# Graph attention with residual and layer norm on one core: node features cut on chip by ScalarE, and fewer, longer transfers for codes and run ends

## The chip, the cores and the metric

The kernel runs on one core of one Trainium2 chip. The metric is the device time of one execution in microseconds. Three runs of the kernel before took 2470.12 to 2475.89 us, the median is 2471.67 us.

## The reference

A graph of N = 6250 nodes with 128 features each and E = 200,000 edges, sorted by their target node `dst`; each edge has 64 features. Attention with 8 heads of 16:

```python
q, k, v = x @ Wq + bq, x @ Wk + bk, x @ Wv + bv            # by node, 8 heads x 16
scores  = sum(q[dst] * k[src], by head) * 0.25 + (edge_attr @ We + be)
e       = exp(scores - segment_max(scores, dst)[dst])
probs   = e / (segment_sum(e, dst) + 1e-10)[dst]
agg     = segment_sum(probs * v[src], dst)
out     = layernorm(x + agg @ Wo + bo)
```

## The kernel before, in words

The edges are cut into tiles of 128. A block is 28 tiles, 14 of each of two halves; a half covers at most 64 nodes, so a block covers two windows of W = 64 nodes. There are NB = 57 blocks, 54 of them full. A full block is worked off in 7 steps of QUAD = 4 tiles; there are 392 steps in all.

First a table of keys and values (`kv_table`, 1 KB for each node) is computed and stored in HBM. Block 0's keys and values are computed directly from gathered rows `x_first`, which are turned into `xt_first`. Then comes the main loop. It is written out for all slots v, without loops in the program; one slot does one step of the block that is entering. Each engine has its own order of work in a slot, and semaphores join them.

- POOL (`gather`, L521) fetches the rows of `kv_table` by source node, one indirect DMA of 128 rows for each tile, four in a step. From block 6 on it is held back: the gathers of step q wait until step q - 2 has been spread and matched, and until an equally old sum is done.
- PE spreads the queries to the edges (`spread_q`, L1228), makes 0/1 matrices of node by edge from codes (`match`, L1205 and L1211), and sums weighted values by node for the block 12 slots behind (`sum_step`, L1265).
- ACT copies the 0/1 matrices out of PSUM (`copy_hots`, L611, or L615 where a slot has one kind only), and in the same order of work does exponentials, copies of weights (L652), and the copies of the block that is being finished.
- DVE multiplies and reduces (L846, L857), weighs the values (L867), and does the maxima by runs and the normalisation.

What is done once in a block falls on fixed slots of its turn. `chain(v, k)` is the block whose scores were complete k slots ago, `at_node(v, k)` the block whose sums were complete k slots ago; with 7 slots to a block, `chain(v, 2)` and `at_node(v, 4)` fall on the same slots, called here the third slot of a turn. In the third slot ACT runs `copy_hots(v)`, `copy_turned` (L660, PSUM to `agg_t`), `copy_weights`; PE runs `spread_q`, `edge_terms` (L1240), `match`, `sum_step`, and last `finish_rows` (L1317 to L1319), which waits for `agg_t` and adds x from `xt_blk`. In PE's order of work the next slot's `spread_q` comes behind `finish_rows`. `fold_halves` and `add_folded` (L977) stand in the first slot of a turn, `leave_over` (L1307) at the head of the second.

SP issues the regular transfers in a loop over blocks b: edge features of b + 1 (`load_edges`, 1 MB), the two windows of turned x of b + 3 (`load_x`, L411 and L412: for each window the first node is loaded into a register, then 128 partitions x 256 bytes are fetched from `x_t` in HBM), the codes of b + 1 (`load_codes`, L422, one transfer for each half), the run ends of b + 1 (`load_seq`, L450), and the results of b - 3 (`store`, L460). The loop is paced by the waits of `load_seq` (for `s_drop`) and of `store` (for the normalised rows).

`xt_blk` has 7 buffers. It is read by `project_q`, three blocks ahead of use, and by `finish_rows`.

Of the kernel before, what the change touches and what calls it, by code (L numbers as in the profile page):

```python
# [5 lines left out]
P = 128  # L6
# [8 lines left out]
QUAD = 4  # L15
# [25 lines left out]
def graph_attention(nc, x_t, x_perm, x_rows, src, dst, src_blk, dst_blk, dst_chk, dst_ends, dst_row, dst_seq, edge_blk, edge_t,  # L41
# [35 lines left out]
    assert NH <= ROWS <= P  # L77

    ENDS = dst_seq.shape[0]
    assert NB <= ENDS <= P  # L80
    STAGES = 6
    GP, NCH, NNB = P, NT, -(-N // P)
# [13 lines left out]
    with ctx:  # L96
        def sb(name, shape, dt=F32):
            return ctx.enter_context(nc.sbuf_tensor(name, shape, dt))
# [6 lines left out]

        kv_table = nc.dram_tensor("kv_table", [NR, KV], F32).ap()
        far_table = nc.dram_tensor("far_table", [ENDS, SEQ], F32).ap()
        code_table = nc.dram_tensor("code_table", [KNOWN, dst_row.shape[0] * HALF[0] * P], BF16).ap()


        ident = sb("ident", [P, P])
# [14 lines left out]
        hots = sb("hots", [P, 2, 2, QUAD * W])  # L126
        edge_f = sb("edge_f", [2 * EF, 2, EPAIRS * P])
        terms_t = sb("terms_t", [P, EPAIRS // EGROUPS * P])
        x_first = sb("x_first", [P, T, D])
        xt_first = sb("xt_first", [P, 2, QUAD * P])  # L130
        src_i = sb("src_i", [P, NT], I32)
        neg_rel = sb("neg_rel", [P, NT])
        base_bc = sb("base_bc", [P, NH])
# [12 lines left out]
        cand = sb("cand", [P, 2, H * T])  # L146
        ends = sb("ends", [P, 2, 2, H])

        seq_far = sb("seq_far", [H, 2, SEQ + 1])
        seq_left = sb("seq_left", [H, 2])  # L150
        seq_b = sb("seq_b", [H, SEQ])
        drop = sb("drop", [H, 1])
# [31 lines left out]
            return kv_buf[0:parts, half, slot:slot + -(-(n + at) // KV), :].rearrange("p a b -> p (a b)")[:, at:at + n]  # L184

        xt = in_kv(P, 1, 0, NR)
        row_i = in_kv(ROWS, 0, 20, ROW + 1).bitcast(I32)
        CODE_HOME = (8, 20)
        row_code = kv_buf[0:ROWS, 0, CODE_HOME[0]:CODE_HOME[1], :].rearrange("p a b -> p (a b)").bitcast(BF16)[:, 0:KNOWN * ROW].rearrange(
# [74 lines left out]
        s_endsdst, s_fartable = sem("s_endsdst"), sem("s_fartable")  # L264
        s_table = [sem(f"s_table{i}") for i in range(STAGES)]
        s_edge = [sem(f"s_edge{i}") for i in range(2)]
        s_x = [sem(f"s_x{i}") for i in range(XBUF)]
        s_kv = [[sem(f"s_kv{i}_{g}") for g in range(SLOT)] for i in range(NBUF)]
        s_y = sem("s_y")

# [22 lines left out]
        s_byedge = sem("s_byedge")  # L293
        s_product, s_dot = sem("s_product"), sem("s_dot")
        s_weighted, s_beside, s_summed = sem("s_weighted"), sem("s_beside"), sem("s_summed")
        s_newq, s_qcopied = sem("s_newq"), sem("s_qcopied")
        s_changes, s_runends = sem("s_changes"), sem("s_runends")
        s_terms, s_termscopied = sem("s_terms"), sem("s_termscopied")
# [97 lines left out]
        def _(sync):  # L396
# [5 lines left out]
            sync.dma_start(src_i[:, T:NT], src_blk[:, T:NT]).then_inc(s_src, 16)  # L402
            sync.dma_start(ends_dst, dst_seq).then_inc(s_endsdst, 16)
            sync.wait_ge(s_rowcode, ROWCODE["squares"])
            sync.dma_start(code_table.rearrange("k (r e) -> r k e", e=ROW), row_code).then_inc(s_codetable, 16)

            def load_x(b):
                if b >= XBUF:
                    sync.wait_ge(s_wo, b - XBUF + 1)
                for j in range(2):  # L410
                    first = sync.value_load(first_row[0:1, 2 * b + j:2 * b + j + 1], min_val=0, max_val=N)  # L411
                    sync.dma_start(xt_blk[:, b % XBUF, j * W:(j + 1) * W], x_t[:, bass.ds(first, W)]  # L412
                                   ).then_inc(s_x[b % XBUF], 16)

            def load_codes(b):
                if b >= CBUF:
                    last = (b - CBUF) * SLOT + GS[b - CBUF] - 1
                    sync.wait_ge(s_matched, HOTS_TO[last + SLOT + LAG])
                n = HALF[b] * P
                for j in range(2):  # L420
                    row = 2 * b + j
                    sync.dma_start(codes[j * KNOWN:(j + 1) * KNOWN, b % CBUF, 0:n], code_table[:, row * ROW:row * ROW + n]  # L422
                                   ).then_inc(s_code[b % CBUF], 16)

            sync.wait_ge(s_win, WIN["last"])
            for b in range(min(XAHEAD, NB)):
# [17 lines left out]
                sync.dma_start(edge_f[:, b % 2, 0:n], edge_blk[:, FIRST_PAIR[b] * P:FIRST_PAIR[b] * P + n]  # L444
                               ).then_inc(s_edge[b % 2], 16)

            def load_seq(b):
                if b >= 2:
                    sync.wait_ge(s_drop, b - 1)
                sync.dma_start(seq_far[:, b % 2, 0:SEQ], far_table[b:b + 1, :].to_broadcast([H, SEQ])  # L450
                               ).then_inc(s_seqi[b % 2], 16)

            def store(b):
                sync.wait_ge(s_normal, b + 1)
# [8 lines left out]
            with sync.If(general == 0):  # L463
                for b in range(NB + 3):
                    if b == 0:
                        load_seq(0)
                        load_edges(0)
                    if b + 1 < NB:
                        load_edges(b + 1)
                    if b + XAHEAD < NB:  # L470
                        load_x(b + XAHEAD)
                    if b + 1 < NB:
                        load_codes(b + 1)
                        load_seq(b + 1)
                    if b >= 3:
                        store(b - 3)
                sync.wait_ge(s_y, 32 * NB)
            with sync.Else():
                for b in range(min(XAHEAD, NB)):
                    sync.wait_ge(s_x[b], 32)  # L480
                sync.wait_ge(s_code[0], 32)
                turn = sync.alloc_register("turn_sp")
                sync.reg_mov(turn, 0)
                with sync.Fori(0, NNB) as b:
                    after(sync, "sp", s_gnode, b + 1)
                    sync.dma_start(xt_blk[:, 0, :], x_t[:, bass.ds(b * P, P)]).then_inc(s_gx, 16)
                    with sync.Fori(0, NCH) as c:
                        r = sync.snap(turn, min_val=0, max_val=NNB * NCH)
                        after(sync, "sp", s_gfree, r + 1)
                        for to, frm in ((g_src, src), (g_dst, dst)):  # L490
                            sync.dma_start(to, frm[bass.ds(c * GP, GP)].rearrange("(p a) -> p a", a=1)
                                           ).then_inc(s_gload, 16)
                        sync.dma_start(g_edge, edge_t[:, bass.ds(c * GP, GP)]).then_inc(s_gload, 16)
                        sync.reg_add(turn, turn, 1)
                    after(sync, "sp", e_dve, b * len(EDVE) + EDVE["normal"])
                    sync.dma_start(out[bass.ds(b * P, P), :], y_out[:, 0, :]).then_inc(s_gy, 16)
                    after(sync, "sp", s_gy, b * 16 + 16)
# [58 lines left out]
        def _(act):  # L556
# [62 lines left out]
            def copy_terms(b):  # L619
                n = PADDED[b] // EGROUPS * P  # L620
                act.wait_ge(s_terms, b + 1)
                if b >= 1:
                    act.wait_ge(s_eterms, b)
                act.activation(terms_t[:, 0:n], ps_e[:, 0:n], ACT.Identity, bias=be_col[:, 0:1]
                               ).then_inc(s_termscopied, 1)

            def copy_q(b):
                act.wait_ge(s_newq, b + 1)
                if b >= QBUF:
                    act.wait_ge(s_byedge, FIRST[b - QBUF + 1])  # L630
                act.copy(q_blk[:, b % QBUF, :], new_q).then_inc(s_qcopied, 1)
# [43 lines left out]
            with act.If(general == 0):  # L675
                for b in range(min(QBUF, NB)):
                    copy_q(b)
                copy_hots(-1)
                for v in SLOTS:
                    if v in HOTS_TO:  # L680
                        copy_hots(v)
                    if chain(v, 4) is not None:
                        exponentials(chain(v, 4))
                    if chain(v, 6) is not None and chain(v, 6) + QBUF < NB:
                        copy_q(chain(v, 6) + QBUF)
                    if at_node(v, 4) is not None:
                        copy_turned(at_node(v, 4))
                    if at_node(v, 5) is not None:
                        copy_projected(at_node(v, 5))
                    if step_in(v - SLOT - LAG) is not None:  # L690
                        copy_weights(step_in(v - SLOT - LAG))
                    if chain(v, -4) is not None:
                        copy_terms(chain(v, -4))
                    if at_node(v, 7) is not None:
                        inverse_deviation(at_node(v, 7))
# [24 lines left out]
        def _(dve):  # L720
# [5 lines left out]
                dve.memset(less_c[:, k:k + 1], less)  # L726
            dve.memset(carried[:, :], 0.0)
            dve.memset(seq_left[:, 1:2], GFAR)
            dve.memset(seq_far[:, :, SEQ:SEQ + 1], FAR)
            dve.memset(base_f[:, NH:NH + 1], float(N))  # L730
            dve.memset(base_f[:, 0:1], 0.0).then_inc(s_const, 1)
            dve.memset(codes[:, :, :].rearrange("p i e -> p (i e)").bitcast(F32), ONES_BF16).then_inc(s_const, 1)
# [187 lines left out]
                                ).then_inc(s_endvals, 1)  # L920

            def crossing_maxima(b):
                far, left = seq_far[:, b % 2, :], seq_left[:, (b + 1) % 2:(b + 1) % 2 + 1]
                dve.wait_ge(s_endsturned, b + 1)
                dve.wait_ge(s_seqi[b % 2], 16 * (b // 2 + 1))

                dve.tensor_tensor_scan(turned_ends, far[:, 0:SEQ], turned_ends, left, ALU.add, ALU.max  # L927
                                       ).then_inc(s_seqf, 1)
# [207 lines left out]
        def _(pe):  # L1136
# [59 lines left out]
            def match(v):  # L1196
# [3 lines left out]
                if bynode is not None:  # L1200
                    b, g = STEPS[bynode]
                    t0, t1 = STEP[b][g]
                    if g == 0:
                        pe.wait_ge(s_code[b % CBUF], 32 * (b // CBUF + 1))
                    one = pe.matmul(ps_t[:, 0:(t1 - t0) * W], node_code[:, :], codes[:, b % CBUF, t0 * W:t1 * W],  # L1205
                                    start=True, stop=True)
                if byedge is not None:
# [85 lines left out]
                pe.transpose(turned_drop, drop[:, :], ident[0:H, 0:H]).then_inc(s_cross, 1)  # L1293

            def project_q(b):
                pe.wait_ge(s_x[b % XBUF], 32 * (b // XBUF + 1))
                if b >= QBUF:
                    pe.wait_ge(s_weights, b - QBUF + 1)
                elif b >= 1:
                    pe.wait_ge(s_qcopied, b)  # L1300
                pe.matmul(new_q, ones[0:1, :], bias_row[:, 0:D], start=True, stop=False)
                pe.matmul(new_q, xt_blk[:, b % XBUF, :], w_qkv[:, 0:D], start=False, stop=True).then_inc(s_newq, 1)
# [161 lines left out]
```

## Time and profile before

| what | value |
|---|---|
| median of 3 runs | 2471.67 us |
| profiled execution | 2468.41 us, span of its instructions 2466.6 us |
| granted TensorE clock, mean | 0.61 of 2.4 GHz |
| PE matmul busy | 1519.7 us (62%) |
| VectorE busy | 1347.9 us (55%) |
| ScalarE busy | 433.9 us (18%) |
| GpSimd busy | 1500.4 us (61%) |
| mean share of the DMA engines | 288.49 MB moved, 117 GB/s |

No engine is busy all the time. To read the profile one has to look at what ended the idle time in front of a group of instructions: "remote" is a wait whose releaser the profile doesn't show, "issue" one in which nothing was waited for that it shows. The ends of matmuls are modelled.

### The profile page before, as it was taken

Reading aid. Unit: us, or ns where it says so; the run is one execution under the profiler, and the core shown is the slowest. Engines: PE = TensorE matmul, PEld = TensorE weight load, DVE = VectorE, ACT = ScalarE, POOL = GpSimd, SP = SyncE. Lnnn points to the kernel's source line nnn. Section 1 sums busy time; section 2 is a strip of 40 time slices with the busy share of each in tenths; the row PEclk is TensorE's granted clock in tenths of the full one; section 3 lists DMA queues with packets and bytes.
Section 4 is the critical chain, followed back from the end, with each engine's and each line's share of the span. In section 5 each row is a group of like instructions: output and inputs, shape, how many; then the busy total and the mean of one; then the engine's idle time right before and its main releaser. Section 6 shows DMA issues by size and latency. Waiting matters only on the chain.

```text
span 2466.6 us, 31372 instructions
## 1 busy us (share of the span) xinstructions
PE 1519.7 (62%) x9783; PEld 1006.6 (41%) x9783; DVE 1347.9 (55%) x3156; ACT 433.9 (18%) x1439; POOL 1500.4 (61%) x1572
## 2 busy tenths in 40 slices
PE   5365465655666656666566666565755655666667
PEld 4233343433444434444343444343433443443444
DVE  4255565555555555555555555555556555555556
ACT  1011121111111111112111111111111111111212
POOL 4726546666666666666666666666666666666661
PEclk7656676656565566555656556556556566655555
DMA  6523334343434334343434343434343343434330
GB/s 247 161 78 104 97 100 127 108 129 109 126 109 121 113 108 127 108 129 109 125 110 127 108 129 109 128 108 126 109 122 114 111 125 109 129 110 124 108 109 23
DMA packets 115165, 288.49 MB, mean 117 GB/s; under 512 B 45909, under 2 KB 53856, under 8 KB 107960
## 3 DMA queue, kind: packets, MB, share of 16 engines
q0 software_dynamic: 74624, 203.26, 28.1%
q1 hardware_dynamic: 37628, 76.52, 9.5%
q10 hardware_dynamic: 2748, 6.69, 0.7%
q8 instruction: 81, 1.33, 0.2%
q14 instruction: 84, 0.69, 0.1%
HBM read 274.69 MB, written 11.67 MB: 116 GB/s over the span
## 4 chain that ended last, share of the span: by engine, by line
another core or an unknown queue 23%; PE 21%; POOL 21%; issue 18%; DVE 12%; DMA 4%; ACT 1%; DVEq 1%; ACTq 0%; POOLq 0%
POOL kv_buf L521 21%; PE q_banks L1228 7%; PE ps_a L1265 4%; DMA kv_buf<-kv_table,src_i 4%; DVE prod L846 3%; DVE score L857 2%; DVE wv L867 1%; PE ps_e L1249 1%; PE ps_t L1205 1%; DVE ps_s L927 1%; PE ps_a L1307 1%; PE ps_t L1211 1%; DVE run_fwd L909 1%; DVE seq_b L933 1%
## 5 line engine op out<-in xcount | busy, mean ns | idle before, releaser
L521 POOL DMA_INDIRECT kv_buf<-kv_table,src_i x1536 | 1470.8, 958 | 910.0 <-issue 405.9
L1228 PE MATMUL q_banks<-q_blk,hots 64*128 64x128 f32 x3128 | 443.6, 427 | 412.5 <-issue 205.7
L1228 PEld LDWEIGHTS q_banks<-q_blk,hots 64*128 64x128 f32 x3128 | 342.2, 295 | 528.0 <-issue 486.1
L611 ACT ACTIVATE hots<-ps_t 128x512 f32<-128x512 f32 x377 | 225.1, 597 | 1821.4 <-remote 1211.6
L846 DVE TENSOR_TENSOR prod<-q_banks,kv_buf 128x512 f32<-128x512 f32 (+1 forms) x392 | 268.9, 686 | 435.4 <-remote 272.9
L867 DVE TENSOR_TENSOR wv<-kv_buf,ps_w 128x512 f32<-128x512 f32 (+1 forms) x392 | 266.4, 680 | 356.0 <-remote 263.7
L1265 PE MATMUL ps_a<-wv,hots 128*64 128x136 f32 x3128 | 414.3, 408 | 4.2 <-issue 2.5
L1265 PEld LDWEIGHTS ps_a<-wv,hots 128*64 128x64 f32 x3128 | 263.2, 198 | 73.4 <-issue 63.1
L857 DVE TENSOR_REDUCE score<-prod 128x32 f32<-128x512 f32 (+1 forms) x392 | 267.3, 682 | 7.7
L1307 PE MATMUL ps_a<-sums_sb,carry_from 128*1 128x136 f32 x112 | 34.1, 406 | 340.4 <-DVE sums_sb L977 295.1
L1307 PEld LDWEIGHTS ps_a<-sums_sb,carry_from 128*1 128x1 f32 x112 | 4.8, 81 | 367.7 <-DVE sums_sb L977 317.8
L1211 PE MATMUL ps_t<-node_code,codes 128*128 128x128 bf16 x782 | 151.4, 292 | 1.2 <-ACT hots L615 1.2
L1205 PE MATMUL ps_t<-codes,node_code 128*128 128x256 bf16 (+1 forms) x392 | 146.6, 374 | 0.0
L927 DVE TENSOR_TENSOR_SCAN ps_s<-seq_far,seq_left,ps_s 8x512 f32<-8x512 f32 x57 | 72.7, 1275 | 116.8 <-remote 71.0
L1211 PEld LDWEIGHTS ps_t<-node_code,codes 128*128 128x128 bf16 x782 | 99.4, 128 | 26.5 <-ACT hots L615 2.1
L652 ACT COPY wv<-weight 128x32 f32<-128x32 f32 (+1 forms) x392 | 96.5, 246 | 0.0
L1205 PEld LDWEIGHTS ps_t<-codes,node_code 128*128 128x128 bf16 x392 | 42.7, 109 | 120.6 <-issue 116.0
L1317 PE MATMUL ps_a<-bias_row,ones 1*128 1x128 f32 x114 | 31.3, 359 | 92.1 <-ACT agg_t L660 70.3
L1240 PE MATMUL ps_e<-edge_f,w_e 128*32 128x512 f32 (+1 forms) x456 | 76.1, 747 | 0.0
L977 DVE TENSOR_TENSOR sums_sb<-ps_a,sums_sb 1x136 f32<-1x136 f32 x57 | 16.9, 297 | 101.7 <-remote 99.6
L933 DVE TENSOR_TENSOR_SCAN seq_b<-seq_far,ps_s 8x512 f32<-8x512 f32 x57 | 68.3, 1198 | 0.0
L1317 PEld LDWEIGHTS ps_a<-bias_row,ones 1*128 1x128 f32 x114 | 19.1, 209 | 107.3 <-ACT agg_t L660 81.5
(155 smaller groups left out, 1485.2 us busy)
## 6 DMA issues: line engine op xcount, KB each, us to landing
edge_f<-in_edge_blk SPq DMA_DIRECT2D x55, 1024.0 KB
kv_buf<-kv_table,src_i POOLq DMA_INDIRECT x1536
kv_table<-kv_buf ACTq DMA_DIRECT2D x12, 512.0 KB, 2.7
xt_blk<-in_x_t SPq DMA_DIRECT2D x114, 32.0 KB
out<-y_out SPq DMA_DIRECT2D x114, 32.0 KB
kv_buf<-in_x_perm SPq DMA_DIRECT2D x5, 512.0 KB
codes<-code_table SPq DMA_DIRECT2D x108, 10.5 KB
code_table<-kv_buf SPq DMA_DIRECT2D x1, 1344.0 KB
```

Source lines behind the costliest of these rows:

```text
L521: pool.indirect_dma_start(kv_buf[:, b % NBUF, t, :], None, kv_table, bass.IndirectOffsetOnAxis(ap=src_i[:, column:column + 1], axis=0)).th ...
L611: one = act.activation(hots[:, v % 2, :, :].rearrange("p k n -> p (k n)"), ps_t[:, :], ACT.Relu, bias=1.0)
L652: act.copy(wv[:, q % 2, 0:t1 - t0, D:WV], by_head(weight[:, b % 2, :], TILES[b])[:, :, t0:t1].rearrange("p h t -> p t h")).then_inc(s_besi ...
L846: dve.tensor_tensor(prod[:, q % 2, 0:n * D].rearrange("p (k j d) -> p j k d", j=2, d=D), q_banks[:, :, 0:n // 2 * D].rearrange("p j (k d) ...
L857: dve.tensor_reduce(score[:, b % 2, :, t0:t1].rearrange("p h t -> p t h"), prod[:, q % 2, 0:(t1 - t0) * D].rearrange("p (t h d) -> p t h d ...
L867: dve.tensor_tensor(wv[:, q % 2, 0:t1 - t0, 0:D].rearrange("p t (h d) -> p t h d", d=HD), kv_buf[:, b % NBUF, t0:t1, D:KV].rearrange("p t ...
L927: dve.tensor_tensor_scan(turned_ends, far[:, 0:SEQ], turned_ends, left, ALU.add, ALU.max).then_inc(s_seqf, 1)
L933: dve.tensor_tensor_scan(seq_b[:, ::-1], far[:, 1:SEQ + 1][:, ::-1], turned_ends[:, ::-1], FAR, ALU.add, ALU.max).then_inc(s_seqb, 1)
L1205: one = pe.matmul(ps_t[:, 0:(t1 - t0) * W], node_code[:, :], codes[:, b % CBUF, t0 * W:t1 * W], start=True, stop=True)
L1211: one = pe.matmul(ps_t[:, QUAD * W + k * P:QUAD * W + (k + 1) * P], codes[:, b % CBUF, t0 * W + k * P:t0 * W + (k + 1) * P], node_code[:, ...
L1228: one = pe.matmul(ps_q[j][:, k * D:(k + 1) * D], hots[own, (v - 1) % 2, 0, k * P:(k + 1) * P], q_blk[own, b % QBUF, :], start=True, stop=True)
L1265: one = pe.matmul(sums(b)[own, :], hots[:, (v - 1) % 2, 1, u * W:(u + 1) * W], wv[:, q % 2, u, :], start=(t0 + u < 2), stop=False)
```

## The change

Four edits. (1) The whole of turned x, 128 partitions x 6378 numbers, is loaded once into the buffer `xt_all`, when block 0's `x_first` (which now lies in the same memory) has been used. From block 3 on, `load_x` is gone from SP's loop; instead ACT, in the third slot of each turn, between `copy_hots` and `copy_turned`, loads the two first nodes into a register and copies 128 x 64 numbers each from `xt_all` to `xt_blk` (`copy_x`). `project_q` waits for a semaphore of ACT. `xt_first` now lies in `prod`. (2) `code_table` has the three code rows of a half beside each other, and the codes of both halves of a block are fetched by one transfer of six rows. (3) The run ends of two blocks are fetched by one transfer. (4) The waits on `s_code` count 16 for a block, not 32.

```diff
@@ sizes and tables
+    TOGETHER = 2
-        code_table = nc.dram_tensor("code_table", [KNOWN, dst_row.shape[0] * HALF[0] * P], BF16).ap()
+        code_table = nc.dram_tensor("code_table", [dst_row.shape[0], KNOWN * HALF[0] * P], BF16).ap()
-        x_first = sb("x_first", [P, T, D])
-        xt_first = sb("xt_first", [P, 2, QUAD * P])
+        xt_all = sb("xt_all", [P, max(N + P, T * D)])
-        seq_far = sb("seq_far", [H, 2, SEQ + 1])
+        seq_far = sb("seq_far", [H, 2, TOGETHER * SEQ + 1])
+        xt_first = prod[:, :, 0:QUAD * P]
+        x_first = xt_all[:, 0:T * D].rearrange("p (t d) -> p t d", t=T)
@@ sync
-            sync.dma_start(code_table.rearrange("k (r e) -> r k e", e=ROW), row_code).then_inc(s_codetable, 16)
+            sync.dma_start(code_table.rearrange("r (k e) -> r k e", e=ROW), row_code).then_inc(s_codetable, 16)
             def load_x(b):
-                if b >= XBUF:
-                    sync.wait_ge(s_wo, b - XBUF + 1)
...
             def load_codes(b):
...
-                for j in range(2):
-                    row = 2 * b + j
-                    sync.dma_start(codes[j * KNOWN:(j + 1) * KNOWN, b % CBUF, 0:n], code_table[:, row * ROW:row * ROW + n]
-                                   ).then_inc(s_code[b % CBUF], 16)
+                sync.dma_start(codes[0:2 * KNOWN, b % CBUF, 0:n],
+                               code_table[2 * b:2 * b + 2, :].rearrange("r (k e) -> (r k) e", e=ROW)[:, 0:n]
+                               ).then_inc(s_code[b % CBUF], 16)
-            def load_seq(b):
-                if b >= 2:
-                    sync.wait_ge(s_drop, b - 1)
-                sync.dma_start(seq_far[:, b % 2, 0:SEQ], far_table[b:b + 1, :].to_broadcast([H, SEQ])
-                               ).then_inc(s_seqi[b % 2], 16)
+            def load_seq(i):
+                if i >= 2:
+                    sync.wait_ge(s_drop, (i - 1) * TOGETHER)
+                ends_of = far_table.rearrange("(i r) s -> i (r s)", r=TOGETHER)[i:i + 1, :]
+                sync.dma_start(seq_far[:, i % 2, 0:TOGETHER * SEQ], ends_of.to_broadcast([H, TOGETHER * SEQ])
+                               ).then_inc(s_seqi[i % 2], 16)
@@ the sync loop over b
-                    if b + XAHEAD < NB:
-                        load_x(b + XAHEAD)
+                    if b == 0:
+                        sync.wait_ge(s_xtcopied, GS[0])
+                        sync.dma_start(xt_all[:, 0:N + P], x_t).then_inc(s_xall, 16)
                     if b + 1 < NB:
                         load_codes(b + 1)
-                        load_seq(b + 1)
+                        if (b + 1) % TOGETHER == 0:
+                            load_seq((b + 1) // TOGETHER)
@@ scalar
+            def copy_x(b):
+                if b == XAHEAD:
+                    act.wait_ge(s_xall, 16)
+                if b >= XBUF:
+                    act.wait_ge(s_wo, b - XBUF + 1)
+                for j in range(2):
+                    first = act.value_load(first_row[0:1, 2 * b + j:2 * b + j + 1], min_val=0, max_val=N)
+                    one = act.copy(xt_blk[:, b % XBUF, j * W:(j + 1) * W], xt_all[:, bass.ds(first, W)])
+                one.then_inc(s_xcopied, 1)
@@ the scalar loop over slots, behind copy_hots(v)
+                    if chain(v, 2) is not None and chain(v, 2) + XAHEAD < NB:
+                        copy_x(chain(v, 2) + XAHEAD)
@@ tensor
             def project_q(b):
-                pe.wait_ge(s_x[b % XBUF], 32 * (b // XBUF + 1))
+                if b < XAHEAD:
+                    pe.wait_ge(s_x[b], 32)
+                else:
+                    pe.wait_ge(s_xcopied, b - XAHEAD + 1)
```

## Rows read from the trace of the kernel before

**Rows 1.** The page: busy us, share of the span and instructions of each engine.

```profile
PE 1519.7 (62%) x9783; PEld 1006.6 (41%) x9783; DVE 1347.9 (55%) x3156; ACT 433.9 (18%) x1439; POOL 1500.4 (61%) x1572
```

**Rows 2.** The page: costliest groups; busy, mean ns of one, idle before and releaser.

```profile
L521 POOL DMA_INDIRECT kv_buf<-kv_table,src_i x1536 | 1470.8, 958 | 910.0 <-issue 405.9
...
L611 ACT ACTIVATE hots<-ps_t 128x512 f32<-128x512 f32 x377 | 225.1, 597 | 1821.4 <-remote 1211.6
```

**Rows 3.** Busy us by engine in two stretches; last columns PEclk, DMA share, GB/s.

```profile
140.00:170.00 30.00, 22.03 (x128) 12.89 (x128) 22.23 (x47) 6.45 (x18) 0.00 (x0) 0.56 0.23 77
1000.00:1400.00 400.00, 252.59 (x1619) 166.02 (x1615) 222.17 (x515) 70.58 (x235) 255.52 (x268) 0.58 0.40 119
```

**Rows 4.** Timeline, POOL quiet: start us, us, engine, line, operation, idle before.

```profile
156.25 0.38 ACT L615 ACTIVATE hots<-ps_t 128x256 f32<-128x256 f32 x1 [1.69 <-PE ps_t L1205]
...
158.35 0.38 ACT L615 ACTIVATE hots<-ps_t 128x256 f32<-128x256 f32 x1 [1.72 <-PE ps_t L1205]
```

**Rows 5.** Timeline of one block's turn, mid-run (columns as in rows 4).

```profile
1213.43 0.42 PE L1211 MATMUL ps_t<-node_code,codes 128*128 128x128 bf16 x2
...
1217.99 0.00 SPq L444 DMA_DIRECT2D edge_f<-in_edge_blk  x1
...
1218.73 0.60 ACT L611 ACTIVATE hots<-ps_t 128x512 f32<-128x512 f32 x1 [7.02 <-issue]
...
1220.86 1.81 SPq L412 DMA_DIRECT2D xt_blk<-in_x_t  x2
1222.43 0.30 DVE L977 TENSOR_TENSOR sums_sb<-ps_a,sums_sb 1x136 f32<-1x136 f32 x1 [3.99 <-remote]
1222.62 0.95 POOL L521 DMA_INDIRECT kv_buf<-kv_table,src_i  x1 [1.81 <-remote]
1222.72 0.65 SPq L422 DMA_DIRECT2D codes<-code_table  x2
...
1222.78 0.61 PE L1307 MATMUL ps_a<-sums_sb,carry_from 128*1 128x136 f32 x2 [7.29 <-DVE sums_sb L977]
...
1231.30 0.69 DVE L846 TENSOR_TENSOR prod<-q_banks,kv_buf 128x512 f32<-128x512 f32 x1 [0.17 <-remote]
1231.44 0.60 ACT L611 ACTIVATE hots<-ps_t 128x512 f32<-128x512 f32 x1 [5.58 <-remote]
1231.93 0.26 ACT L660 COPY agg_t<-ps_a 128x128 f32<-128x128 f32 x1
...
1232.24 0.48 PE L1317 MATMUL ps_a<-bias_row,ones 1*128 1x128 f32 x2 [2.48 <-ACT agg_t L660]
...
1233.90 1.22 PE L1228 MATMUL q_banks<-q_blk,hots 64*128 64x128 f32 x8
```

**Rows 6.** Line L660: who waited for it, us in all and times.

```profile
L660 ACT COPY agg_t<-ps_a x57: 259/259/267, 240.1 to 2457.3; 128x128 f32<-128x128 f32 x57
...
  PE ps_a L1317: 70.3, 40
```

**Rows 7.** Line L390, the one register load outside SP: duration ns min/median/max.

```profile
L390 ACTq TENSOR_LOAD <-general_i x1: 470/470/470, 103.1 to 103.1; - x1
...
L390 ACTq FUSED_REGOPS  x1: 181/181/181, 103.6 to 103.6; - x1
...
L390 ACTq SEQ_ASSERT  x1: 25/25/25, 103.8 to 103.8; - x1
```

**Rows 8.** Line L411, SP's register loads: duration ns min/median/max.

```profile
L411 SPq TENSOR_LOAD <-first_row x114: 2/270/713, 17.0 to 2306.1; - x114
```

**Rows 9.** SP's DMA issues at the start of the main loop (columns as in rows 4).

```profile
108.21 1.44 SPq L444 DMA_DIRECT2D edge_f<-in_edge_blk  x2
116.69 9.80 SPq L412 DMA_DIRECT2D xt_blk<-in_x_t  x2
127.19 1.40 SPq L422 DMA_DIRECT2D codes<-code_table  x2
```

**Rows 10.** DMA issues by line: KB each.

```profile
xt_blk<-in_x_t SPq DMA_DIRECT2D x114, 32.0 KB
```

More of the change, by code:

```diff
@@ L79, in graph_attention @@
     ENDS = dst_seq.shape[0]
+    TOGETHER = 2
+    assert ENDS % TOGETHER == 0
     assert NB <= ENDS <= P
@@ L266, in graph_attention @@
         s_edge = [sem(f"s_edge{i}") for i in range(2)]
-        s_x = [sem(f"s_x{i}") for i in range(XBUF)]
+        s_x, s_xall = [sem(f"s_x{i}") for i in range(XAHEAD)], sem("s_xall")
         s_kv = [[sem(f"s_kv{i}_{g}") for g in range(SLOT)] for i in range(NBUF)]
@@ L295, in graph_attention @@
         s_weighted, s_beside, s_summed = sem("s_weighted"), sem("s_beside"), sem("s_summed")
+        s_xcopied = sem("s_xcopied")
         s_newq, s_qcopied = sem("s_newq"), sem("s_qcopied")
@@ L404, in _ @@
             sync.wait_ge(s_rowcode, ROWCODE["squares"])
-            sync.dma_start(code_table.rearrange("k (r e) -> r k e", e=ROW), row_code).then_inc(s_codetable, 16)
+            sync.dma_start(code_table.rearrange("r (k e) -> r k e", e=ROW), row_code).then_inc(s_codetable, 16)
             def load_x(b):
-                if b >= XBUF:
-                    sync.wait_ge(s_wo, b - XBUF + 1)
                 for j in range(2):
                     first = sync.value_load(first_row[0:1, 2 * b + j:2 * b + j + 1], min_val=0, max_val=N)
-                    sync.dma_start(xt_blk[:, b % XBUF, j * W:(j + 1) * W], x_t[:, bass.ds(first, W)]
-                                   ).then_inc(s_x[b % XBUF], 16)
+                    sync.dma_start(xt_blk[:, b, j * W:(j + 1) * W], x_t[:, bass.ds(first, W)]
+                                   ).then_inc(s_x[b], 16)
             def load_codes(b):
@@ L480, in _ @@
                     sync.wait_ge(s_x[b], 32)
-                sync.wait_ge(s_code[0], 32)
+                sync.wait_ge(s_code[0], 16)
                 turn = sync.alloc_register("turn_sp")
@@ L728, in _ @@
             dve.memset(seq_left[:, 1:2], GFAR)
-            dve.memset(seq_far[:, :, SEQ:SEQ + 1], FAR)
+            dve.memset(seq_far[:, :, TOGETHER * SEQ:TOGETHER * SEQ + 1], FAR)
             dve.memset(base_f[:, NH:NH + 1], float(N))
@@ L922, in crossing_maxima @@
             def crossing_maxima(b):
-                far, left = seq_far[:, b % 2, :], seq_left[:, (b + 1) % 2:(b + 1) % 2 + 1]
+                i, r = divmod(b, TOGETHER)
+                far, left = seq_far[:, i % 2, r * SEQ:(r + 1) * SEQ + 1], seq_left[:, (b + 1) % 2:(b + 1) % 2 + 1]
                 dve.wait_ge(s_endsturned, b + 1)
-                dve.wait_ge(s_seqi[b % 2], 16 * (b // 2 + 1))
+                dve.wait_ge(s_seqi[i % 2], 16 * (i // 2 + 1))
                 dve.tensor_tensor_scan(turned_ends, far[:, 0:SEQ], turned_ends, left, ALU.add, ALU.max
@@ L1203, in match @@
                     if g == 0:
-                        pe.wait_ge(s_code[b % CBUF], 32 * (b // CBUF + 1))
+                        pe.wait_ge(s_code[b % CBUF], 16 * (b // CBUF + 1))
                     one = pe.matmul(ps_t[:, 0:(t1 - t0) * W], node_code[:, :], codes[:, b % CBUF, t0 * W:t1 * W],
```

## The prediction

> **What bounds the kernel now.** I read the page first: no engine is busy for more than about six tenths of the span [rows 1]. So the end is set by waits, and the next view is the groups with the idle time before them. POOL is the nearest to a bound. Its 1536 gathers take 1470.8 us, and 405.9 us more are the 0.3 us between one gather and the next ("issue") [rows 2]. Both together, 1877 us in 384 steps, are 4.9 us for each step. In the main loop a turn of seven steps is paid with more than that: in the 400 us from 1000 on, 268 gathers were made, or 67 steps, at 5.97 us for each step [rows 3]. So 1.1 us in each step, or 7.5 us in each turn, are POOL's waits for PE (its gathers are tied to steps that are two behind).
>
> Why is PE late? Two stretches tell. While POOL is quiet, one step follows the other in 2.1 us (158.35 less 156.25) [rows 4], and ACT's copy of the matrices comes right after the matmul that makes them. With gathers running, the matmul L1211 stood at 1213.43 to 1213.85 in the timeline, but ACT's copy that waits for nothing else started at 1218.73, 4.9 us later [rows 5]. The profile names no releaser for most of ACT's idle time there: 1211.6 us of 1821.4 us are "remote" [rows 2]. The granted clock doesn't explain it, since it is the same in both stretches (0.56 and 0.58, so mostly the 1.2 GHz level) [rows 3]. PE's signals are thus seen late when gathers run, by an amount that the trace doesn't explain, and POOL's waits are the price. I can't work out this part, and it is the largest uncertainty: a change to SP's or ACT's load may move it.
>
> Inside a turn one place is plain. In the third slot ACT copies the matrices (1231.44), then `agg_t` (1231.93), and PE, idle for 2.48 us, starts `finish_rows` at 1232.24 on that very copy. The next `spread_q` follows at 1233.90, when its other inputs have been there for almost 2 us (the product started at 1231.30 and took 0.69 us, the matrices were copied at 1232.04) [rows 5]. PE waited so in 40 of 57 turns, 70.3 us in all [rows 6]. Whatever is put before `agg_t` on ACT is put before PE's next step.
>
> **The change part by part.**
>
> *ACT's new work.* In 54 turns ACT makes two register loads and two copies between the matrices and `agg_t`. A register load on ACT is seen once: 470 + 181 + 25 = 676 ns [rows 7], so 1.35 us for two. ACT's order puts the first copy behind the first load and beside the second. The last copy is exposed; it is half as wide as the copy of 128x128, which takes 259 ns [rows 6], and I take 0.26 us for it. The loads can begin when the copy of the matrices has started, and `agg_t` started 0.49 us after it [rows 5]. So `agg_t` moves from 0.49 to 1.35 + 0.26 = 1.61 us behind, or 1.1 us later. From both sides: with SP's median load of 270 ns [rows 8] it is 2 x 0.27 + 0.26 - 0.49 = 0.3 us; with SP's pace in the middle of the run, where two loads with their transfers were up to 1.5 us apart (1.81 us from the first issue to the end of the second) [rows 5], it is 2 x 1.5 + 0.26 - 0.49 = 2.8 us. I take 1.1 us, since it is the one value from ACT's own rows. What is queued behind on ACT is `agg_t` and `copy_weights`; the first has PE waiting, the second is needed only a slot later.
>
> *How much of it reaches the end.* PE waited in 40 of 57 turns, so in 38 of 54: 38 x 1.1 = 42 us. In the other turns PE was the later one and the cost is hidden there. Of the 42 us a part comes back, because POOL pauses while PE is late and PE's signals come faster when POOL pauses. The bounds are nothing and all; I take three quarters, since `spread_q` had nothing else to wait for [rows 5]: 31 us.
>
> *SP's removed work.* Out of each turn go two register loads, two transfers of 32 KB [rows 10], one of the two for the codes, and half of one for run ends. None of them has a waiter in this trace: x is loaded three blocks ahead, and SP then waits for the rows of an older block. The DMA engines are at 0.40 [rows 3]. I take nothing for it as a gain. Its bounds are in the rival below, since POOL, DVE and PE were all idle while SP issued them [rows 5].
>
> *The weight of the small pieces.* The x transfers write 256 bytes in each partition (32 KB over 128) [rows 10]. The Trainium skill, "DMA: Bandwidth & Descriptors", section "Specifications", says that transfers below 512 bytes do not reach line rate because each needs a read as well. By that rule taking them away would free more of the DMA engines than their bytes say; no row here prices it, and at a share of 0.40 I would still not count it. It speaks for the faster rival.
>
> *The one large load.* 128 x 6378 x 4 bytes are 3.27 MB. At the 119 GB/s that the loop moves [rows 3] on top of the loop's own traffic that is up to 27 us. SP issues it behind the two edge loads, at about 110 us, in place of x of block 3, whose issue took from 116.69 to 126.49 [rows 9]. At that time the loop proper has not begun, and POOL falls silent from 134 on for want of buffers (it is idle in 140 to 170 [rows 3]). The codes of block 1 go out behind it and are needed at the seventh slot, after 150. Taken as hidden; if the cover fails, 5 to 13 us once.
>
> *Code table, run ends, waits.* The table is written in runs three times as long and read by half as many transfers. The run ends come one or two blocks earlier than needed. The waits on PE change only their count. Together nothing.
>
> Sum against the profiled execution: 2468.4 + 31 = 2499 us. The runs' median lies 3.3 us over that execution, so 2503 us is forecast for the median.
>
> **The rivals.**
>
> *Hidden.* PE's lateness with gathers running (4.9 us in the row above) swallows the 1.1 us: PE's signals come in POOL's pauses anyway. For it speaks that most idle time on ACT is "remote"; against it, that PE's wait for `agg_t` is named and is direct. Time: 2472 us.
>
> *Faster, the other side.* SP's issuing is itself part of what makes the signals late. Between 1217.99 and 1223.4 SP issued edges, x and codes. DVE's `add_folded` came 3.99 us late at 1222.43, POOL resumed at 1222.62 after 1.81 us, PE at 1222.78 after 7.29 us [rows 5]: all within 0.4 us, near the end of SP's burst. If the shorter burst takes off two thirds of POOL's 1.81 us in each of 54 turns, 65 us go; less the 31 us of ACT it is -34 us: 2438 us. It decides from 0.6 us for each turn on. Against it: ACT's copy at 1231.44 was also late (5.58 us idle) with SP silent. With all of the 1.81 us the time would be 2405 us.
>
> *Much slower.* ACT's register loads take what SP's take beside gathers, 2.8 us in place of 1.1, and all turns pay: 54 x 2.8 = 151 us, 2620 us.
>
> *The change doesn't do what it says* (x is still fetched for each block) can be excluded: the transfers are gone from SP's loop for all but three blocks.
>
> **How the numbers follow.** Forecast 0.39 (its own range 2480 to 2540, from 38 x 0.3 us to 54 x 1.3 us), much slower 0.09, hidden 0.21, faster 0.31. A change of under 0.2% (5 us) can't be told from none. So slower 0.48, same 0.21, faster 0.31. The range, 2428 to 2545, holds the forecast and the hidden case and most of the faster one; it leaves out the much slower case and the lower end of the faster one.
>
> **What would show it.** In the changed kernel, `agg_t` should start about 1.6 us after the matrices in the third slot, not 0.49; PE's idle time in front of L1317's successor should grow from 70 us towards 110 us, with ACT as releaser; the time of a turn should grow by about 0.6 us, in all turns alike; `project_q` should never wait for ACT's copy. The hidden case shows the same move of `agg_t` and an unchanged turn. The faster case shows a shorter idle time of DVE before `add_folded` and of POOL at the head of the turn. A register load far from 0.68 us on ACT would make the forecast wrong in size; a turn that is shorter although `agg_t` is later would make it wrong in kind.

## The result, and the profile after

The changed kernel took 2494.39 us (median of 19 runs, 2481.87 to 2505.37), the kernel before 2472.46 us beside it (19 runs, 2463.71 to 2484.72). The ratio is 1.0087, 95% interval 1.0072 to 1.0103: 22 us slower, where 31 us slower was forecast. The profiled execution took 2500.54 us, 32 us more than that of before.

The experiments ran on four chips on which the kernel before takes 2024 to 2026 us and the change, timed on one of them, costs 7 us. Which chip gave this result is not known by number; "the first chip" stands below for that chip, or for the state it was in. The experiments show why the change costs 7 us on the others. For the 22 us here there are only this run's own trace and what carries over.

The page of the change, costliest groups (columns as in [rows 2]):

```profile
L526 POOL DMA_INDIRECT kv_buf<-kv_table,src_i x1536 | 1465.7, 954 | 947.4 <-issue 406.6
...
L616 ACT ACTIVATE hots<-ps_t 128x512 f32<-128x512 f32 x377 | 225.1, 597 | 1808.0 <-remote 1157.4
```

One gather costs what it did, 0.95 us. POOL's idle time grew from 910.0 [rows 2] to 947.4 us. The loop's middle, as in [rows 3]:

```profile
1000.00:1400.00 400.00, 239.21 (x1598) 159.17 (x1598) 217.29 (x508) 75.27 (x257) 249.95 (x263) 0.64 0.38 113
```

There are 263 gathers in 400 us where there were 268 [rows 3]. TensorE was busy for 13.4 us less, with 21 matmuls fewer and at a granted clock of 0.64 in place of 0.58. Over the whole run:

```profile
PE 1496.3 (60%) x9783; PEld 991.7 (40%) x9783; DVE 1346.6 (54%) x3156; ACT 460.9 (18%) x1547; POOL 1495.2 (60%) x1572
```

ACT has 27.0 us more to do than in [rows 1]; the 108 copies of 0.244 us are 26.4 us of it. PE has the same matmuls and is busy for 23.4 us less. Where ACT's new work stands is seen in the timeline of one turn (columns as in [rows 4]):

```profile
1246.68 0.60 ACT L616 ACTIVATE hots<-ps_t 128x512 f32<-128x512 f32 x1 [6.88 <-remote]
...
1247.30 0.24 ACT L639 COPY xt_blk<-xt_all 128x64 f32 x1
...
1248.21 0.24 ACT L639 COPY xt_blk<-xt_all 128x64 f32 x1 [0.66 <-issue]
1248.36 0.26 ACT L675 COPY agg_t<-ps_a 128x128 f32<-128x128 f32 x1
...
1248.67 0.79 PE L1338 MATMUL ps_a<-bias_row,ones 1*128 1x128 f32 x2 [4.62 <-ACT agg_t L675]
```

`agg_t` starts 1.68 us after the matrices here. The median over the 57 blocks, taken from the start times of L675 and of the L616 before each, is 1.40 us; it was 0.49. Who waits for it:

```profile
L675 ACT COPY agg_t<-ps_a x57: 257/258/265, 244.8 to 2489.8; 128x128 f32<-128x128 f32 x57
...
  PE ps_a L1338: 153.4, 53
```

In [rows 6] that was 70.3 us in 40 turns. None of TensorE's waits is put down to the copy of x itself. The register load is short and even, and has three parts (duration in ns, min/median/max):

```profile
L638 ACTq TENSOR_LOAD <-first_row x108: 271/273/291, 166.4 to 2388.5; - x108
L638 ACTq FUSED_REGOPS  x108: 147/147/157, 166.7 to 2388.8; - x108
L638 ACTq SEQ_ASSERT  x108: 18/18/18, 166.9 to 2389.0; - x108
```

From the 61st to the 376th copy of the matrices (starts of the `hots` copies, 45 turns of seven slots) a turn takes 42.42 us where it took 41.86. That is 0.56 us a turn, or 30 us in 54 turns.

### The profile page after: what moved, and what is told of

Same layout as the page of the kernel before. It is cut to its first block, busy times and chain, and to the rows that moved or that the text cites. A ratio compares the mean times of both kernels' runs of the same rounds, so it can differ in the third digit from the quotient of the medians.

```text
span 2498.7 us, 31180 instructions
## 1 busy us (share of the span) xinstructions
PE 1496.3 (60%) x9783; PEld 991.7 (40%) x9783; DVE 1346.6 (54%) x3156; ACT 460.9 (18%) x1547; POOL 1495.2 (60%) x1572
## 2 busy tenths in 40 slices
DMA packets 99051, 288.21 MB, mean 115 GB/s; under 512 B 30149, under 2 KB 38096, under 8 KB 91592
## 3 DMA queue, kind: packets, MB, share of 16 engines
q1 hardware_dynamic: 21516, 76.25, 8.9%
## 4 chain that ended last, share of the span: by engine, by line
another core or an unknown queue 28%; PE 23%; POOL 17%; issue 15%; DVE 10%; DMA 3%; ACT 2%; ACTq 1%; DVEq 1%; POOLq 0%
POOL kv_buf L526 17%; PE q_banks L1246 7%; PE ps_a L1283 4%; DMA kv_buf<-kv_table,src_i 3%; DVE score L874 2%; DVE prod L863 2%; PE ps_t L1223 1%; PE ps_t L1229 1%; DVE run_fwd L926 1%; PE ps_a L1338 1%; DVE wv L884 1%; PE ps_a L1328 1%; PE ps_a L1339 1%; PE ps_s L1310 1%
## 5 line engine op out<-in xcount | busy, mean ns | idle before, releaser
L526 POOL DMA_INDIRECT kv_buf<-kv_table,src_i x1536 | 1465.7, 954 | 947.4 <-issue 406.6
L616 ACT ACTIVATE hots<-ps_t 128x512 f32<-128x512 f32 x377 | 225.1, 597 | 1808.0 <-remote 1157.4
L1283 PE MATMUL ps_a<-wv,hots 128*64 128x136 f32 x3128 | 404.8, 401 | 4.6 <-issue 2.1
L1283 PEld LDWEIGHTS ps_a<-wv,hots 128*64 128x64 f32 x3128 | 257.5, 194 | 73.1 <-issue 61.7
L995 DVE TENSOR_TENSOR sums_sb<-ps_a,sums_sb 1x136 f32<-1x136 f32 x57 | 16.9, 297 | 106.0 <-remote 103.9
```

The costliest lines, as they stand in the source:

```text
L526: pool.indirect_dma_start(kv_buf[:, b % NBUF, t, :], None, kv_table, bass.IndirectOffsetOnAxis(ap=src_i[:, column:column + 1], axis=0)).th ...
L616: one = act.activation(hots[:, v % 2, :, :].rearrange("p k n -> p (k n)"), ps_t[:, :], ACT.Relu, bias=1.0)
L1283: one = pe.matmul(sums(b)[own, :], hots[:, (v - 1) % 2, 1, u * W:(u + 1) * W], wv[:, q % 2, u, :], start=(t0 + u < 2), stop=False)
```

## The experiments

The ratios are to the kernel before, run on the same chip between the others. Times are medians.

| kernel | chip | this us | before us | ratio, 95% interval |
|---|---|---|---|---|
| copy of x last in the slot | 12 | 2027.08 | 2026.32 | 1.0001, 0.9993 to 1.0010 |
| the same | 5 | 2025.84 | 2024.50 | 1.0006, 0.9996 to 1.0015 |
| the same | 10 | 2025.55 | 2025.22 | 1.0002, 0.9993 to 1.0011 |
| codes and run ends merged only | 12 | 2027.45 | 2026.32 | 1.0007, 0.9998 to 1.0016 |
| the same | 10 | 2026.25 | 2025.22 | 1.0004, 0.9995 to 1.0013 |
| no copy of x | 12 | 2027.26 | 2026.32 | 1.0001, 0.9992 to 1.0010 |
| both ways of x | 12 | 2034.63 | 2026.32 | 1.0039, 1.0025 to 1.0053 |
| the change again | 5 | 2031.15 | 2024.50 | 1.0034, 1.0021 to 1.0046 |
| register loads three times | 5 | 2135.78 | 2024.50 | 1.0551, 1.0529 to 1.0572 |
| before, no gathers | 5 | 1638.48 | 2024.50 | 0.8090, 0.8079 to 0.8101 |
| the change, no gathers | 4 | 1637.19 | 2024.09 | 0.8087, 0.8076 to 0.8098 |
| copy last, no gathers | 4 | 1637.09 | 2024.09 | 0.8084, 0.8073 to 0.8095 |

**Copy of x last in ScalarE's slot.** The call is moved behind the copies that TensorE waits for:

```diff
                     if v in HOTS_TO:
                         copy_hots(v)
-                    if chain(v, 2) is not None and chain(v, 2) + XAHEAD < NB:
-                        copy_x(chain(v, 2) + XAHEAD)
...
                     if at_node(v, 7) is not None:
                         inverse_deviation(at_node(v, 7))
+                    if chain(v, 2) is not None and chain(v, 2) + XAHEAD < NB:
+                        copy_x(chain(v, 2) + XAHEAD)
```

> All of the change is kept, but the copy of x stands last in ScalarE's slot, behind the copies that TensorE waits for. Theory A (the place of the copy costs: it holds agg_t back in front of finish_rows, and nothing else of the change moves the time): 2472 us, agg_t 0.5 us after the matrices, TensorE's wait for agg_t back at 70 us. Theory B (the change would gain by what it takes from SyncE and the queues, and the place of the copy hides that): about 2450 us or less. Theory C (ScalarE's 0.96 us a block costs wherever it stands, or the cost is elsewhere in the change): 2490 to 2495 us.

Measured on two more chips:

> The changed kernel with ScalarE's copy of x last in its slot, beside the unaltered change. On a chip of 2026 us as before, 1.000. On a chip where the kernel before takes 2472 us: theory A 1.000 (2472), theory B below 0.995 (the removed issues on SyncE show only where signals come late), theory C 1.009 as the change.

> The changed kernel with the copy of x last in ScalarE's slot, once more, for the case that this falls on a chip where the kernel before takes 2472 us; the change there is 1.009 of before. Theory A (the place of the copy): 1.000, 2472 us. Theory B (fewer issues on SyncE also make the late signals less late): 0.995 or less. Theory C (the rest of the change costs where signals are late): 1.004 to 1.009. On a chip of 2025 us it says nothing new: 1.000.

All three are within 0.1% of before. In the profile, PE's wait for `agg_t` is small again (view of line L675 in the run on chip 5):

```profile
L675 ACT COPY agg_t<-ps_a x57: 258/260/265, 136.1 to 2014.4; 128x128 f32<-128x128 f32 x57
...
  PE ps_a L1338: 8.5, 36
```

The change as it is takes 7 us more than before on chip 5 (below), and this kernel, on the same chip, at most 3 us. On these chips, then, the place of the copy is the whole cost that can be measured, and theories B and C fall. On the first chip this kernel was not run.

**Codes and run ends only.** SyncE loads x as in the kernel before; `copy_x` and `xt_all` are gone:

```diff
-                    if b == 0:
...
-                        sync.dma_start(xt_all[:, 0:N + P], x_t).then_inc(s_xall, 16)
+                    if b + XAHEAD < NB:
+                        load_x(b + XAHEAD)
```

> Only the codes of both halves by one transfer and the run ends of two blocks by one; x's columns are loaded by SyncE's two transfers a block as in the kernel before. Theory A: 2472 us, within 0.3%. Theory B: about 2455 us, part of a gain by fewer issues on SyncE. Theory C with the cost in these two parts: 2480 to 2495 us.

> Codes and run ends merged, x loaded as before, once more for a chip where the kernel before takes 2472 us. Theory A: 1.000. Theory B: 0.993 to 0.999. Theory C: 1.004 to 1.009. On a chip of 2025 us: 1.000.

1.0007 and 1.0004: half the transfers for codes and for run ends neither gain nor cost here.

**No copy of x.** This kernel leaves out the columns of x for blocks 3 on; TensorE reads those of the first three again.

```diff
-                    if chain(v, 2) is not None and chain(v, 2) + XAHEAD < NB:
-                        copy_x(chain(v, 2) + XAHEAD)
...
-                else:
-                    pe.wait_ge(s_xcopied, b - XAHEAD + 1)
...
-                pe.matmul(new_q, xt_blk[:, b % XBUF, :], ...)
+                pe.matmul(new_q, xt_blk[:, b % XAHEAD, :], ...)
```

> The changed kernel without ScalarE's copies and TensorE's wait for them; TensorE reads the columns of the first three blocks again and again, so the copying of x for blocks 3 on is left out. The large transfer of x, the merged codes and run ends stay. Theory A (the copy on ScalarE is the whole cost): 2472 us, within 0.3%. Theory B (fewer issues on SyncE gain by themselves): 2438 to 2450 us. Theory C (the cost is not the copy): above 2485 us.

1.0001. The large load and SyncE's shorter list of work are in this kernel, and ACT's work is not: what SyncE no longer does is worth nothing here, and the large load costs nothing.

**Both ways of x.** As codes and run ends only, with the large load and `copy_x` in its place of the change, writing to a spare buffer:

```diff
-                    one = act.copy(xt_blk[:, b % XBUF, j * W:(j + 1) * W], xt_all[:, bass.ds(first, W)])
+                    one = act.copy(xt_spare[:, 0, j * W:(j + 1) * W], xt_all[:, bass.ds(first, W)])
```

> Merged codes and run ends, SyncE's loads of x kept as in the kernel before and used, and beside them x on chip and ScalarE's register loads and copies in their place of the change, into a buffer that nothing reads; TensorE waits for both. Theory A (ScalarE's place in front of agg_t): 2494 us, the same as the change. Theory B (SyncE's removed work is a gain that the change has and this kernel has not): above 2500 us, by what the no-copy kernel is below 2472. Theory C (the cost comes of SyncE's moved issues or of the columns arriving by another way): 2472 us.

2034.63 us: 8 us, and not 22. The sign fits theory A. The size didn't: it was expected for a kernel of 2472 us, and the kernel before took 2026 us here.

**The change again, on such a chip.**

> The changed kernel unaltered, on whichever chip this falls. The four kernels before this one ran on a chip on which the kernel before takes 2026 us, not 2472, with the same mean of every instruction, and in its profile nobody waits for a signal that was given microseconds ago. Theory A (ScalarE's 0.9 us in front of agg_t, passed on where agg_t is the last link): on such a chip 2034 us (1.004, as with both ways of x together), since GpSimd's gathers bound the step there and leave slack beside TensorE; on a chip of 2472 us, 2494 (1.009). Theory C (the 22 us come of something else in the change): 1.000 on the chip of 2026 us.

1.0034, or 7 us, as theory A said. Its interval and that of both ways of x (on another chip) overlap, so SyncE's removed work again shows no gain. Line L675 in this run:

```profile
L675 ACT COPY agg_t<-ps_a x57: 257/258/265, 137.4 to 2020.2; 128x128 f32<-128x128 f32 x57
...
  PE ps_a L1338: 55.8, 55
```

PE's wait grew by 47 us over the kernel with the copy last, and the time by 5. The groups of the change on this chip show what hides the rest:

```profile
L526 POOL DMA_INDIRECT kv_buf<-kv_table,src_i x1536 | 1464.9, 954 | 478.9 <-issue 428.1
...
L616 ACT ACTIVATE hots<-ps_t 128x512 f32<-128x512 f32 x377 | 225.1, 597 | 1412.6 <-PE ps_t L1229 1412.6
```

POOL is busy with gathers or with the 0.30 us between two of them for 1893 us, and waits for little else (50.8 us in all, before the loop too). A turn of 28 gathers by (0.954 + 0.30) us is 35.1 us; the measured turn is 35.31 us, and 35.26 with the copy last. GpSimd sets the turn, and PE has slack.

**How large the slack is: register loads three times.**

```diff
-                    first = act.value_load(first_row[0:1, 2 * b + j:2 * b + j + 1], min_val=0, max_val=N)
+                    for _ in range(3):
+                        first = act.value_load(first_row[0:1, 2 * b + j:2 * b + j + 1], min_val=0, max_val=N)
```

> The changed kernel with each of ScalarE's two register loads a block done three times, about 2 us more in front of agg_t (agg_t 3.4 us after the matrices). On a chip of 2472 us: theory A with the slope of the change (0.6 us passed on of 0.9) 65 us more, 2560; on a chip of 2026 us, slack used up at first and then one for one: 57 blocks by 2 us is 112 us, at 60 to 100% is 70 to 110 us more, 2100 to 2145. A rival (the copy costs by its presence, not by its length): less than 10 us over the change.

2135.78 us, 104.6 more than the change, at the upper end for such a chip. The median start of `agg_t` is 3.52 us after the matrices, 2.12 us more than in the change. The turn is 37.40 us, 2.09 us more: nearly all is passed on. The first 0.91 us of delay cost 0.05 us of a turn in these profiles (0.10 us by the medians, 5.3 us in 54 turns) and the next 2.12 us cost almost all of themselves, so the slack was 0.8 to 0.9 us. That POOL pays for it is in its waits (view of line L526: first the change, then this kernel, both on chip 5):

```profile
  PE q_banks L1246: 37.5, 100
```

```profile
  PE q_banks L1247: 146.3, 126
```

109 us more, about the 105 us of the time. The rival "by its presence, not by its length" is out.

**No gathers.** In `gather(b)`:

```diff
                         if b >= HELD and t == t0 + 2:
                             pool.wait_ge(s_summed, q - AHEAD - SLOT - LAG)
+                        if b >= HELD:
+                            continue
```

VectorE's wait is changed to count only the gathers that are left.

> The kernel before without its gathers of K and V from block 6 on (that part of the computation is left out; the buffers keep old rows). If the gathers on GpSimd bound the step: far less, at TensorE's and ScalarE's own chain, 1700 us or less on a chip of 2026 us; and if the gathers are what makes signals late on a chip of 2472 us, about the same 1700 us there. If the chain through TensorE, ScalarE and VectorE bounds it, less than 5% is gained on a chip of 2026 us, and on a chip of 2472 us what the gathers have to do with late signals shows.

1638 us: the gathers bind the step on these chips, by 387 us. On the first chip it was not run, so whether the gathers make its signals late stays open.

**The change, and the copy last, without gathers.** The same lines added to both:

> The changed kernel without its gathers of K and V from block 6 on (that part of the computation is left out). The kernel before without them took 1638 us where before took 2025, ratio 0.809. Theory A (the 0.9 us in front of agg_t cost what the gathers do not hide: with them 7 us of 52, because each turn of 28 gathers by 1.255 us is 35.1 us anyway): most of it shows now, 54 turns by 0.5 to 0.9 us is 27 to 49 us more, 1665 to 1687, ratio 0.823 to 0.834. Rival (the 7 us on chips of 2025 us are what the copy costs, whatever else bounds the step, and the 22 us of the first chip have another cause): 1645, ratio 0.813.

> The same without gathers, with ScalarE's copy of x last in its slot. Theory A: back at the kernel before without gathers, 1638 us, ratio 0.809, within 5 us. A rival (ScalarE's 0.96 us a block costs wherever it stands once nothing hides it): 1665 or more.

The last one came out as theory A had it. The first did not: 1637.19 us, no cost at all, where at least 27 us were expected; and the rival's 7 us are not there either. The delay is present. Line L677 is the `agg_t` copy, first in the change, then with the copy last:

```profile
L677 ACT COPY agg_t<-ps_a x57: 258/259/267, 136.7 to 1621.7; 128x128 f32<-128x128 f32 x57
...
  PEld ps_a L1340: 75.6, 56
  PE ps_a L1340: 61.3, 55
```

```profile
L677 ACT COPY agg_t<-ps_a x57: 258/259/266, 137.4 to 1626.4; 128x128 f32<-128x128 f32 x57
...
  PEld ps_a L1340: 27.0, 56
  PE ps_a L1340: 12.6, 54
```

PE waits 49 us longer, and the kernel takes the same time. The delay isn't lost in slack. From PE's L1330 at the head of a turn to the first `spread_q` behind `finish_rows` the change takes 10.59 us and the kernel with the copy last 9.87; from there to the next head it takes 16.70 and 17.44 (medians of 40 turns). So 0.72 us of a turn are lost in the first part and 0.74 us regained in the second.

Where PE gets them back shows in the middle of the run (columns as in [rows 3]; the change, then the copy last):

```profile
300.00:1500.00 1200.00, 925.84 (x7522) 620.86 (x7520) 1005.38 (x2369) 353.63 (x1188) 0.00 (x0) 0.81 0.13 43
```

```profile
300.00:1500.00 1200.00, 996.04 (x7517) 666.31 (x7513) 1010.45 (x2369) 348.96 (x1188) 0.00 (x0) 0.75 0.13 43
```

The same matmuls, about 7520, took 925.8 us at a granted clock of 0.81 and 996.0 us at 0.75. In 2 us slices of one turn, later than its wait for `agg_t` (at 891 us in both), the change:

```profile
898.62:900.62 2.00, 2.00 (x15) 1.54 (x13) 1.93 (x12) 0.16 (x2) 0.00 (x0) 0.53 0.03 8
900.62:902.62 2.00, 2.00 (x14) 1.43 (x12) 1.97 (x4) 1.13 (x4) 0.00 (x0) 0.61 0.00 0
902.62:904.62 2.00, 2.00 (x22) 1.46 (x21) 1.24 (x3) 0.50 (x2) 0.00 (x0) 1.00 0.01 4
904.62:906.62 2.00, 1.88 (x23) 1.28 (x21) 2.00 (x5) 1.12 (x5) 0.00 (x0) 1.00 0.00 0
```

and with the copy last:

```profile
900.32:902.32 2.00, 2.00 (x13) 1.63 (x12) 1.97 (x8) 1.13 (x4) 0.00 (x0) 0.50 0.00 0
902.32:904.32 2.00, 2.00 (x12) 1.43 (x10) 1.18 (x2) 0.00 (x0) 0.00 (x0) 0.50 0.01 4
904.32:906.32 2.00, 2.00 (x15) 1.29 (x15) 1.75 (x4) 0.90 (x3) 0.00 (x0) 0.50 0.00 0
906.32:908.32 2.00, 2.00 (x21) 1.40 (x21) 1.70 (x5) 0.70 (x2) 0.00 (x0) 0.80 0.00 0
```

A slice at 0.50 is at 1.2 GHz throughout, one at 1.00 at 2.4 GHz. A slice at 0.53 is at the low level for (1.00 - 0.53) / 0.50 of its 2 us. So the change spends 1.9 + 1.6 = 3.4 us here at the low level, and the kernel with the copy last 2 + 2 + 2 + 0.8 = 6.8. In both kernels PE had stood idle for DVE shortly before, and for the same time: 1.84 us until 898.39 in the change, 1.83 us until 898.81 with the copy last. What differs is its wait for `agg_t` some 7 us earlier, 1.14 us against 0.23 us, and after it the place of PE's work against the clock's changes: the level falls at 898.76 in the change and at 900.27 with the copy last. The two programs differ in the place of the copy alone, so that place does shorten the low level here; how it does so wasn't tested. Over a turn PE is busy for 70.2 us / 44 = 1.6 us less (1200 us are 44 turns), which pays for 0.9 us of waiting for `agg_t` and 0.5 us more for DVE's sums (160.6 us over the run, 134.8 with the copy last). The two turns are equally long, 27.30 us. So the step that A had left out is the clock: here the wait of TensorE was not added to the time, since the work after it was granted more clock. That the two amounts are so nearly equal is not explained by anything measured, and may be luck.

## Why the prediction was right, and where it was not

*Delay of `agg_t`.* Forecast 1.1 us, measured 0.91 (1.40 less 0.49). The mis-sized term is the register load. The one on ACT in [rows 7] took 676 ns; in the loop it is 273 + 147 + 18 = 438 ns. SyncE's median of 270 ns [rows 8] for the first part was the better row. With 438 ns the forecast's own sum would have given 2 x 0.44 + 0.26 - 0.49 = 0.65 us. It counted nothing between the parts, and that is the rest: one further load cost 0.53 us of delay, not 0.44. The two errors offset in part. The same term ends the much slower rival: ACT's loads show none of SyncE's spread, their longest first part is 291 ns.

*Turns that pay.* Forecast 38 of 54, from the 40 turns with a wait [rows 6]. PE waited in 53 of 57, and its wait grew by 83 us, to 153 and not to about 110. A turn where PE came a little too late to wait before does wait once the copy is 0.9 us later. PE may also have come earlier by itself, its work being shorter by 23.4 us.

*Part passed on.* Forecast three quarters of 42 us, 31 us. Measured 0.56 us of 0.91 us in each of 54 turns, or six tenths of 49 us, which is 30 us; 32 us between the profiled executions, 22 between the medians. So the total came near in part by luck: more turns paid than forecast, and less of each was passed on. I had put the rest down to POOL's pauses making the signals come faster. The trace doesn't show that: ACT's copy of the matrices starts more than 1 us after the later of its matmul and ACT's work before it in 199 of 377 cases, and all 377 together start 784 us late (before: 218, 788 us). What it does show is the clock, 0.632 for 0.610, and PE's shorter work. That this is what gave back the rest on the first chip is argued from the runs without gathers, not shown.

*SyncE's removed work, the large load, code table, run ends.* Forecast nothing, and nothing on chips 10 and 12 (1.0001 to 1.0007). Line q1 of the change's queue list has 21516 packets, 16112 fewer than before, and on those chips no time goes with them:

```profile
q1 hardware_dynamic: 21516, 76.25, 8.9%
```

The rule of the Trainium skill, "DMA: Bandwidth & Descriptors", section "Specifications", that pieces below 512 bytes cost a read as well spoke for the faster rival. 15760 of the packets that are gone were below that size (45909 and 30149 by the pages), and no run shows a gain by it.

*The faster rival* needed SyncE's bursts to be what makes signals late. On the first chip the lateness stayed when the bursts went: the waits of the kernel before

```profile
POOL kv_buf L521 <- remote: 309.9, 180, 2.6
...
DVE prod L846 <- remote: 272.9, 96, 37.5
```

stand against these of the change (us in all, times, longest):

```profile
DVE prod L863 <- remote: 366.7, 101, 38.7
...
POOL kv_buf L526 <- remote: 325.8, 190, 2.7
```

VectorE's idle time before `add_folded`, whose fall the prediction named as a sign, went from 101.7 to 106.0 us. The rival is out as a net result; that a small gain of that kind lay under the 22 us was not tested on that chip.

*What bounds the kernel.* Here the prediction named the wrong cause. It saw PE's signals late and tied this to the running gathers. On the other chips the gathers run back to back at 1.25 us and no wait of any of the twelve kernels is put down to "remote". In the change on chip 5, each of the 377 copies of the matrices starts 0.04 us after what it needs. So gathers alone don't make signals late. Late signals are something of the first chip, or of its state in those runs; without them the kernel is bound by GpSimd, at 2025 us. What makes them late stays open: no experiment ran on that chip. It explains why the same 0.91 us cost 22 us there and 7 us elsewhere as far as this: POOL's pauses between gathers, beyond the 0.30 us after each, are 6.7 us of a turn there in the kernel before (from the starts of its gathers; 7.5 us by [rows 3]) and 0.2 us elsewhere, so on the first chip no cover of gathers lies over PE.

That the place of the copy is also the cause of the 22 us on the first chip is argued: the delay of `agg_t` is the same 0.91 us, PE's named wait for it grew by 83 us, and the turn by 0.56 us. No experiment took the delay away there.

No version beat the kernel before. Where ScalarE's copy stands last, all of the change is kept and costs nothing that can be measured on three chips.

## What to carry to other kernels

Work added to an engine costs by what is queued behind it: the same two register loads and copies cost 7 us, and 22 us on the first chip, in front of a copy that TensorE waits for, and nothing at the end of the slot where that was tried. Size it by a row of the same kind in a loop, not by one at the start, and ask of each turn whether the engine would now wait, not whether it waited. Where TensorE spends part of a turn at 1.2 GHz, a new wait of it may cost less or more than its length: compare its busy time and granted clock as well. And before you explain idle time by the kernel, look whether another chip shows it.

## What the runs showed of the hardware

- One program took 2472 us in one place and 2024 to 2026 us on four numbered chips, with a gather of the same length (958 and 954 ns) and a granted clock of 0.61 against 0.68 to 0.70. The clock can be only a small part: in the change TensorE was busy for 76 us more (1496.3 us against 1420.2 on chip 5), and the time is 463 us longer. Most of the difference is in the time from an instruction to those that wait for its signal. Of the 377 copies of the matrices, the median one starts 0.04 us after what it needs on chip 5, and so does the one at 90%; on the first chip, in the kernel before, these are 1.84 and 5.04 us, and the longest is 11.0 us.
- A register load from on-chip memory cost ScalarE 438 ns in each of 108 cases, and one further load in the same place 0.53 us of delay (2.12 us for four).
- Without gathers TensorE waited 49 us more and was done at the same time, at a granted clock of 0.81 and not 0.75 in the middle of the run. With gathers running it went the other way on chip 5: over the run 0.665 to 0.674 in the six runs of the change and 0.680 to 0.702 in the eleven with the copy last. So the same delay went with a higher clock in one case and with a lower one in the other.
